# Graph network on one core: GpSimd copies the next group's indices ahead of the last gather of the present group

## The reference

```
h = relu(layernorm(x))
x = x + L0(h)      # messages h[src] @ W_msg.T + b + embed[type], segment_sum by dst, then a GRU cell
h = relu(layernorm(x))
x = x + L1(h)      # GCN: norm[:, None] * h[src], segment_sum by dst, @ W.T + b, layernorm
h = relu(layernorm(x))
x = x + L2(h)      # relational: per-edge mix of 4 bases, segment_sum by the source end
h = relu(layernorm(x))
x = x + L3(h)      # attention over the edges of a node (softmax by dst), then a projection
```

## Time and profile before

| | us |
|---|---|
| median of 3 timed runs | 10787.66 (10783.5 to 10787.84) |
| profiled execution, its own time | 10766.11 |
| span of the profile | 10764.3 |
| first edge pass, first to last gather issued | 135.4 to 2446.0 |
| second edge pass, first to last gather issued | 2505.5 to 4815.7 |

### The profile page before, as it was taken

How to read it: one execution, slowest core, us unless ns; L and a number is a source line. 1 busy time by engine, 2 the same in 40 slices (tenths; PEclk the granted TensorE clock), 3 DMA queues, 4 the chain that set the end, 5 groups by cost and what they waited for, 6 DMA issues and landing times. The chain is left out here.

```text
span 10764.3 us, 142924 instructions
## 1 busy us (share of the span) xinstructions
PE 7296.1 (68%) x34582; PEld 5598.5 (52%) x34582; DVE 4890.2 (45%) x12591; ACT 1824.8 (17%) x4365; POOL 7100.4 (66%) x7075
## 2 busy tenths in 40 slices
PE   2655556555566666668888888888836666666666
PEld 1444445443333333336777777777624555555555
DVE  5444444445566666663222222222264555555556
ACT  1111111111111111112222222222221111111111
POOL 3666666665666666666888888888816555555553
PEclk6555555555555555556777777777755555555555
DMA  6122221222222222224444444444472222222221
GB/s 237 57 58 57 59 59 57 59 59 60 77 73 76 75 75 77 76 71 64 55 55 55 55 55 55 55 55 55 52 214 68 68 67 69 67 66 68 65 68 50
DMA packets 809415, 765.67 MB, mean 71 GB/s; under 512 B 128472, under 2 KB 701362, under 8 KB 809073
## 3 DMA queue, kind: packets, MB, share of 16 engines
q0 software_dynamic: 375872, 414.65, 21.5%
q1 hardware_dynamic: 340391, 271.94, 8.2%
q10 hardware_dynamic: 92938, 77.03, 2.3%
HBM read 544.72 MB, written 224.78 MB: 71 GB/s over the span
## 5 line engine op out<-in xcount | busy, mean ns | idle before, releaser
L1408 POOL DMA_INDIRECT scat<-msg_out,msg_idx x1564 | 2432.7, 1555 | 491.8 <-issue 421.7
L1997 POOL DMA_INDIRECT soft_rows<-proj,soft_slot x1564 | 1488.0, 951 | 1360.6 <-DVE soft_x L2184 690.2
L723 POOL DMA_INDIRECT L_rows<-H,L_slot x1568 | 1502.0, 958 | 691.3 <-issue 652.4
L988 POOL DMA_INDIRECT L_rows<-H,L_slot x1568 | 1498.2, 955 | 684.5 <-issue 618.0
L1501 PE MATMUL msg_ps_msg<-msg_hb,msg_lhs 128*128 128x128 f32 x6272 | 1600.3, 437 | 1.2 <-DVE msg_lhs L1474 1.2
L1501 PEld LDWEIGHTS msg_ps_msg<-msg_hb,msg_lhs 128*128 128x128 f32 x6272 | 1493.0, 328 | 191.8 <-issue 190.3
L1474 DVE SCALAR_TENSOR_TENSOR msg_lhs<-msg_dst_sp,msg_node,msg_ps_c 128x512 f32<-128x512 f32 x784 | 551.1, 745 | 2056.4 <-ACT msg_dst_sp L1429 2032.6
L859 PE MATMUL L_sum<-L_onehot,L_rows 128*128 128x64 f32 x3136 | 699.8, 394 | 782.9 <-issue 693.5
L859 PEld LDWEIGHTS L_sum<-L_onehot,L_rows 128*128 128x128 f32 x3136 | 648.7, 303 | 865.7 <-issue 851.8
L2126 PE MATMUL soft_ps_sum<-soft_onehot,soft_x 128*128 128x64 f32 x3136 | 753.1, 422 | 317.2 <-DVE sums_b L2243 226.1
L2126 PEld LDWEIGHTS soft_ps_sum<-soft_onehot,soft_x 128*128 128x128 f32 x3136 | 705.5, 328 | 383.9 <-issue 283.7
(11 more groups left out here) (365 smaller groups left out, 10487.9 us busy)
## 6 DMA issues: line engine op xcount, KB each, us to landing
L_rows<-H,L_slot POOLq DMA_INDIRECT x3136
msg_hb<-HB SPq DMA_DIRECT2D x392, 128.0 KB
soft_at_in<-in_edge_attr_dram SPq DMA_DIRECT2D x195, 256.0 KB
scat<-L_zeros SPq DMA_DIRECT2D x64, 408.0 KB
rel_parts<-scat SPq DMA_DIRECT2D x100, 256.0 KB, 5.0
HB<-L_prod ACTq DMA_DIRECT2D x49, 512.0 KB
scat<-msg_out,msg_idx POOLq DMA_INDIRECT x1564
soft_rows<-proj,soft_slot POOLq DMA_INDIRECT x1564
```

The source lines that it names most:

```text
L723: pool.indirect_dma_start(rows[:, k, j, :], None, t["H0"], bass.IndirectOffsetOnAxis(ap=slot[:, k, j:j + 1], axis=0)).then_inc(gathered[k] ...
L988: pool.indirect_dma_start(rows[:, k, j, :], None, t["H1"], bass.IndirectOffsetOnAxis(ap=slot[:, k, j:j + 1], axis=0)).then_inc(gathered[k] ...
L1408: pool.indirect_dma_start(t["scat"][j], bass.IndirectOffsetOnAxis(ap=idx[:, k, j:j + 1], axis=0), out[:, k, j, :], None, compute_op=ALU.ad ...
L1997: pool.indirect_dma_start(rows[:, s % SC, j, :], None, t["proj"], bass.IndirectOffsetOnAxis(ap=slot[:, s, j:j + 1], axis=0)).then_inc(gath ...
```

## The change

In both edge passes POOL's stage gather is split into three. give_indices waits for the ring and copies a group's indices. gather_first waits for that copy and issues the first three gathers. gather_last issues the fourth. The list of stages puts give_indices of the next group (distance 1) between the two others. Nothing else of the program is edited. The wide branch keeps the order of before through in_order.

```diff
-            def gather(i, r, w, s):
+            def give_indices(i, r, w, s):
+                pool.wait_ge(multiplied, r * GB + s + 1)
+                pool.tensor_copy(slot[:, s % R, :], t["src_i"][:, ds((i * GB + s) * J, J)]).then_inc(idx_ready, 1)
+
+            def fetch(i, r, w, s, first, last):
                 k = s % R
-                if empty(i, w, s):
-                    return
-                pool.wait_ge(multiplied, r * GB + s + 1)
-                pool.tensor_copy(slot[:, k, :], t["src_i"][:, ds((i * GB + s) * J, J)]).then_inc(idx_ready, 1)
-                pool.wait_ge(idx_ready, r * GB + s + 1)
-                pool.nop(nofuse=True)
-                for j in range(J):
+                for j in range(first, last):
                     pool.indirect_dma_start(rows[:, k, j, :], None, t["H0"],
                                             bass.IndirectOffsetOnAxis(ap=slot[:, k, j:j + 1], axis=0)
                                             ).then_inc(gathered[k], 16)
-            with_nodes(pool, S, t, [(0, gather)], [])
+
+            def gather_first(i, r, w, s):
+                pool.wait_ge(idx_ready, r * GB + s + 1)
+                pool.nop(nofuse=True)
+                fetch(i, r, w, s, 0, J - 1)
+
+            def gather_last(i, r, w, s):
+                fetch(i, r, w, s, J - 1, J)
+            with_nodes(pool, S, t, [(0, gather_first), (1, give_indices), (0, gather_last)], [],
+                       in_order=[give_indices, gather_first, gather_last])
...
```

## The result

| | before | after |
|---|---|---|
| median, us | 10785.58 (10780.05 to 10801.17, 8 runs) | 10825.83 (10816.2 to 10839.69, 8 runs) |
| ratio after / before | | 1.0036, 95% interval 1.0026 to 1.0047 |
| profiled execution, span | 10764.3 | 10820.1 |
| first edge pass, first to last gather | 2310.6 | 2320.5 |
| second edge pass, first to last gather | 2310.2 | 2333.2 |

Slower by 0.36%, where I had forecast 3.1% faster. The machine was met in two conditions, one in which before takes about 10790 us, as in this table, which I call held, and one in which it takes 9940 us and the changed kernel 9426, which I call free; each experiment is compared with before under its own condition.

A forecast was written before the change was run, and what follows sets the result against it. POOL's gather cadence plus one pause in 7 groups was taken as the bound; 0.47 less 0.045 us over 784 groups gains 333, so 10766.1 becomes 10433, forecast 10455 as medians run 21.6 higher; range 10410 to 10550, with other cases 10405 to 10800.

The forecast's parts named there:

- POOL's gaps: POOL in both edge passes: copy-to-gather gap falls to 0.30, group-to-group gap is 0.30, period 5.20 against 5.67 us.
- That 0.77: Gap on POOL between a group's index copy and the first gather reading it, forecast to become 0.30 us.
- What bounds it: Both edge passes: POOL's cadence plus an occasional pause sets 5.90 us a group, since only POOL's work is alike.
- One pause in 7 groups is what they need: PE and DVE in the edge passes catch up when POOL stands about 1.4 us once in 7 groups, 0.20 a group.
- a pause in 6 groups: After the change consumers need POOL's 1.47 us pause every 6 groups in place of 7, 0.245 us a group.
- The 0.97 us between groups: POOL's index copy (0.20) plus the 0.77 behind it; named as a consumers' rest only in the slower rival.
- the 0.245 of all pauses: Forecast total of POOL's pauses a group after the change, 1.47 / 6, in place of 0.20 us.
- Rival three: Edge passes slower: losing the consumers' rest between groups gives 6.05 us a group, 118 us more, 10905; chance 0.11.
- Rival one: Consumers set the edge passes' pace; each 0.47 returns as ring wait before the copy, 10788; chance 0.18 with another rival.
- the fourth: Rival: POOL's 0.77 gap follows a copy whatever gather comes next, time stays 10788; chance 0.18 together with another rival.
- the mechanism as forecast: POOL's shorter period in both edge passes, less added pauses: 0.425 us a group over 784 groups, 333 us gained.
- the 0.045: Part of POOL's gain a group given back to more frequent pauses, 0.245 in place of 0.20 us.

The follow-up runs named there:

- e2: Changed kernel with three gathers a group in place of four in both edge passes: held, passes 1798.6 and 1844.2 us.
- e3: Changed kernel with two gathers a group in place of four in both edge passes: held, passes 1292.1 and 1651.8 us.
- d2: Changed kernel, first pass with 15 more PE semaphore updates a group, second with a POOL memset behind each copy: held, 10798.3 us, passes 2342.4 and 2316.7.
- e4: Changed kernel, first pass's degree-histogram one-hots made for one tile of edges in place of four, less DVE work: held, 10822.97 us, passes 2322.1 and 2333.4.
- d1: Changed kernel, first pass without 8 of PE's 16 matmuls a group, second with 16 PE nops a group: held, 10781.6 us, passes 2287.5 and 2334.0.
- e1: Changed kernel, both edge passes uncoupled: POOL waits only for its own landings, PE multiplies a constant tile without waiting for gathers: held, 12782 us.

## Why the prediction was wrong, point by point

- **POOL's gaps.** Right in sign, and the gap behind the copy is 0.16 where I took 0.30: a period of 5.06 instead of 5.20. That 0.77 is a wait for the engine's own copy is shown: it vanishes with the distance and does not move.
- **What bounds it.** I took POOL for the pacemaker because two passes with unlike work agreed at 5.90. The agreement was real and its reading wrong. In the held condition both passes agree because what bounds them goes with the number of gathers (1.33 and 1.29 us each in e2 and e3), and hardly with POOL's order of issuing them: 5.90 in both passes before, 5.92 and 5.96 after. The 5.91 of d2 is POOL's own sequence, and shows that the consumers can live with it.
- **The step that failed** is "One pause in 7 groups is what they need", made into "a pause in 6 groups". I had seen that consumers recover behind a pause and took the pauses of 1.4 us for the whole of the rest. The 0.97 us between groups were rest as well. That a stretch without gathers is what they need is shown by d2, where a memset gave one back and the ring waits went. Taken away, that time came back in full: ring waits of 0.66 and 0.68 us a group in place of the 0.245 of all pauses that I had summed. Rival three had this mechanism, at 118 us; it is 40 for the whole kernel and 33 in the two passes. Rival one had the place (each 0.47 comes back in front of line 984's copy) and the size, 10788. I gave rival three 0.11, and rival one together with the fourth 0.18.
- **The number 0.97.** It was in my rows that at 60 us after a pause the consumers took 2 groups in 20 us. A consumer whose own work is 3.7 us and that takes 10 is not late, it is held. That called for a price of the whole gap, not of one pause more.
- **The last 0.36%.** Of the 56 us between the two profiled spans 9.9 lie in the first pass, 23.0 in the second and 17.6 in the attention phase, which nobody edited (2645.5 and 2663.1 us). Those 17.6 are no work of the change: over the nine held traces that phase takes 2645.5 to 2664.5 us, and the trace of before happens to have the shortest. The passes are at the held condition's pace in either order; why the second order meets it 10 to 23 us worse stays open. The difference repeats in the second pass, where e4 and d1 have 2333.4 and 2334.0 with the new order and the code of before took 2310.2 and 2319.1. That the longer pauses do it is a guess that was not tried.
- **In the free condition** the mechanism as forecast carries, though its size is off there too: 516 us, against 333. The consumers never fill the ring, so the 0.045 that I gave back for it was not due, and the gap is 0.14 shorter. By the cadences (5.67 and 5.06) the edit is worth 0.61 us a group, 478 us over 784; where the other 38 lie is not shown, for there is no trace of before there.

**What holds the engines up** is narrowed down and not settled. Shown: gathers do it, whatever else POOL does between them (e1, d2); shorter work of DVE gains nothing (e4), 16 nops a group cost nothing and 8 matmuls less gain 33 us (d1). The traces of the two conditions differ in one more way. Of the 25088 completions by which the first pass's gathers report to their semaphores (16 for each of 1568), the trace of the free condition holds 25007, that of before in the held one 6505, that of the changed kernel 5274, and e1_free's 3475. Completions are also a quantity that stays nearly level in the first pass of the held condition. Counting 64, 48 or 32 a group of gathers and 10 of the node work's DMAs, it is 12.5, 12.6 and 12.7 in a us with 4, 3 and 2 gathers, against 14.5 in the free condition. That is an estimate from the passes' lengths. The same estimate gives 11.7 for e1_free, and with 20 of other DMAs 14.1 and 14.4 for the second pass with 4 and 3 gathers, so there is no one rate that fits all. The path on which completions are counted or recorded is my suspect and no more; the run that was to test it, with 16 completions more a group, met the free condition both times.

The Trainium skill describes such a path in "NOTIFIC — the notification-queue block", section 7.1 "Overflow: three behaviours, one of which stalls the engine": the block that writes out records of instructions and semaphores always pushes back on its producers when its inner buffers fill, and a counter of such stalls, if not zero, "would mean the notification path had throttled an engine". The engines standing in "issue" agree with that. The lost records do not speak for it by themselves: the same section has records dropped where a queue's ring is full, and none lost in the inner buffers. No run here reads that counter. All 8 timed runs of the changed kernel list a granted clock (0.58 to 0.582), so each left records, and whether a run that records nothing is held up as well is not shown.

## What to carry to other kernels

- When idle time of a producer is cut, ask who used it. Here the 0.97 us between groups were a rest in which PE and DVE caught up, and what was taken from it came back as ring waits.
- Two passes with unlike work and the same pace share a bound, but that needn't be the engine that is common to both. To find out, uncouple producer and consumer in one run: e1_free showed what no timeline had told.
- Look for "issue" gaps on engines that have all they need, and compare a kernel with before only in the same condition of the machine. The same edit is worth -5.2% in one and +0.36% in the other.

## What the hardware showed that I had not expected

- In the held condition, while indirect gathers run unbroken, there are stretches in which PE starts one instruction in 1.40 us and DVE's sequencer takes a step in 0.71 us; POOL itself is slowed to 1.40 us a gather on the mean. In the same condition the message phase, with a scatter in 1.86 us, runs as in the free one:

```profile
L1424 POOL DMA_INDIRECT scat<-msg_out,msg_idx x1564: 1546/1555/1667, 4932.2 to 7839.9; - x196
```

```profile
L1424 POOL DMA_INDIRECT scat<-msg_out,msg_idx x1564: 1546/1553/1667, 4260.9 to 7166.1; - x196
```

- The attention phase, whose code is the same, takes 2663.1 us in the held condition and 1975.1 in the free one, 688 us of the 1393 between the changed kernel's two spans. The two edge passes make 641 of them.

```profile
L2013 POOL DMA_INDIRECT soft_rows<-proj,soft_slot x1564: 942/947/1901, 8043.8 to 10706.9; - x196
```

```profile
L2013 POOL DMA_INDIRECT soft_rows<-proj,soft_slot x1564: 940/944/1918, 7370.0 to 9345.1; - x196
```

- A gather of half as many rows takes POOL 0.903 us in place of 0.944, one of half as long rows as long as a whole one:

```profile
L1003 POOL DMA_INDIRECT L_rows<-H,L_slot x1568: 892/903/1146, 2192.8 to 4150.5; - x196
```
